# Row sums of a softmax: from matmuls with ones to a GpSimd fold and a VectorE reduction, in the second of two small-head attention layers

## What is computed

```
x = x + _L1_attn_ref(...)          # l1a: causal attention, 32 heads, 8 key heads, 8 channels a head
...
x = x + _L2_xattn_ref(_layernorm(x, axis=-1), ctx_2048, ctx_2048, mask_BxS2_if1,
                      L2_xattn_w_q, L2_xattn_w_k, L2_xattn_w_v, L2_xattn_w_o, L2_xattn_b_o)   # l2x
x = x + _L2_ffn_ref(_layernorm(x, axis=-1), L2_ffn_w_gate, L2_ffn_w_up, L2_ffn_w_down)        # l2f
```

## Time and profile before

| | us |
|---|---|
| median of 3 runs (1521.43 to 1523.54) | 1522.03 |
| profiled execution, its own time | 1525.09 |
| its span | 1523.3 |
| PE busy in the span | 1372.9 |
| DVE busy | 919.2 |
| ACT busy | 767.3 |
| POOL busy | 528.1 |

### The profile page before, as it was taken

How to read it: one execution, slowest core, us unless ns; L and a number is a source line. 1 busy time by engine, 2 the same in 40 slices (tenths; PEclk the granted TensorE clock), 3 DMA queues, 4 the chain that set the end, 5 groups by cost and what they waited for, 6 DMA issues and landing times.

```text
span 1523.3 us, 24834 instructions
## 1 busy us (share of the span) xinstructions
PE 1372.9 (90%) x9246; PEld 855.1 (56%) x9264; DVE 919.2 (60%) x1713; ACT 767.3 (50%) x1847; POOL 528.1 (35%) x528
## 2 busy tenths in 40 slices
PE   7869999999888879999999998998996789988799
PEld 3434555565455545666667774664663545545536
DVE  7784322224588755545555788855787587686631
ACT  3452111111788567776776456457776455363230
POOL 3230000000277468886882000110843435414200
PEclk9979999999999999999999999998998798988899
DMA  8020211001200300000000100020001100000100
GB/s 257 26 86 1 68 53 41 1 0 60 107 2 2 126 0 8 8 8 8 8 8 1 77 23 1 1 83 2 2 2 72 56 1 2 3 0 3 30 0 28
DMA packets 21851, 48.06 MB, mean 32 GB/s; under 512 B 1506, under 2 KB 16995, under 8 KB 20580
## 3 DMA queue, kind: packets, MB, share of 16 engines
q1 hardware_dynamic: 21732, 46.47, 8.9%
HBM read 41.22 MB, written 5.24 MB: 31 GB/s over the span
## 4 chain that ended last, share of the span: by engine, by line
PE 64%; DVE 21%; ACT 6%; issue 5%; POOL 4%; DMA 0%; DVEq 0%; ACTq 0%; POOLq 0%
PE PS L890 47%; PE PS L1128 5%; DVE work L2638 4%; PE PS L1187 3%; PE PS L891 3%; ACT work L1733 2%; PE PS L987 2%; PE PS L1225 2%; DVE small L2076 2%; DVE small L2425 1%; PE PS L904 1%; DVE work L2222 1%; DVE X L2617 1%; DVE work L2606 1%; POOL work L823 1%
## 5 line engine op out<-in xcount | busy, mean ns | idle before, releaser
L890 PE MATMUL PS<-XT,WB 128*128 128x512 f32 (+1 forms) x688 | 300.8, 595 | 5.2 <-DVE XT L2102 2.9
L890 PEld LDWEIGHTS PS<-XT,WB 128*128 128x128 f32 (+1 forms) x688 | 127.1, 191 | 149.8 <-issue 146.1
L1733 ACT ACTIVATE work<-PS,small 128x128 f32<-128x128 f32 x512 | 137.7, 416 | 43.6 <-DVE small L2425 43.6
L2297 DVE TENSOR_TENSOR work<-PS,work 128x512 f32<-128x512 f32 x48 | 33.1, 691 | 170.1 <-PE PS L890 170.1
L1659 ACT ACTIVATE work<-PS 128x512 f32<-128x512 f32 x48 | 28.7, 597 | 194.6 <-PE PS L890 194.6
L2425 DVE TENSOR_REDUCE small<-PS 128x4 f32<-128x512 f32 x128 | 80.5, 684 | 36.1 <-PE PS L890 34.6
L890 PE MATMUL PS<-XT,WA 128*128 128x512 f32 (+2 forms) x224 | 97.9, 600 | 4.4 <-DVE XT L2102 2.3
L666 POOL TENSOR_SCALAR small<-small 128x4 f32<-128x4 f32 x22 | 5.1, 230 | 268.3 <-DVE small L2079 268.2
L2638 DVE SCALAR_TENSOR_TENSOR work<-PS,vec,work 128x508 f32<-128x508 f32 (+2 forms) x108 | 80.2, 743 | 13.7 <-DVE work L2638 6.5
L1128 PE MATMUL PS<-WB,work 128*128 128x256 f32 x384 | 86.9, 379 | 0.5 <-DVE work L2302 0.5
L890 PE MATMUL PS<-WA,XT 128*128 128x256 f32 (+1 forms) x384 | 81.5, 374 | 3.6 <-DVE XT L2410 1.8
(11 more groups left out here) (388 smaller groups left out, 2988.3 us busy)
## 6 DMA issues: line engine op xcount, KB each, us to landing
WB<-in_l0f SPq DMA_DIRECT2D x8, 768.0 KB, 8.1
WB<-in_l1x SPq DMA_DIRECT2D x1, 6144.0 KB, 18.3
WB<-in_l0f SPq DMA_DIRECT2D x32, 96.0 KB, 7.2
WB<-in_l2f SPq DMA_DIRECT2D x1, 3072.0 KB, 10.0
WA<-in_l3a SPq DMA_DIRECT2D x1, 2624.0 KB, 9.3
WB<-in_l3f SPq DMA_DIRECT2D x1, 2064.0 KB, 7.9
WA<-in_l1f SPq DMA_DIRECT2D x1, 2056.0 KB, 11.2
C<-in_ctx SPq DMA_DIRECT2D x2, 1024.0 KB, 7.1
```

The source lines that it names most:

```text
L890: mm = lambda o, l, r, s, e: nc.tensor.matmul(o, l, r, start=s, stop=e)
L1733: f(wk(12288 + (u % 8) * G + h * P, P), bank(j)[:, h * P:(h + 1) * P], ACT.Exp, bias=sm(704 + (u % 8) * 4 + h, 1)).then_inc(*act_step(*([j ...
L2297: v.tensor_tensor(l0f_h(m)[:, lo:lo + G], bank(j), l0f_s(m)[:, lo:lo + G], ALU.mult).then_inc(*dve_step(j))
```

## The change

In `l2x` the 16 matmuls with ones of each group go, with the window of ones and its write on ACT. POOL makes one fold for each unit (128x512 exponentials to 128x256 sums of two), into columns of `XT` and `WA` that are free then. DVE reduces 64 columns a head of four units at once (128x1024 to 128x16), takes 16 reciprocals, spreads them, copies the product out of PSUM, and multiplies with the inverses of the group before from the bank of this group, as in `l1a`. ACT's exponentials of unit u wait for the fold of unit u-8, whose buffer they take. POOL's fold of unit u, from u = 8 on, waits for the inverses of group (u-8)//4, whose columns it takes. POOL's folds and the steps for `l2f`'s weights are put into one order by hand: the folds of rounds 0 to 7, then one weight step and the folds of one round in turn up to round 16, the folds of round 17, the roots, the folds of rounds 18 to 21. `rb` is now in both layers. The small tiles of sums and reciprocals move from `C` to `work` in both layers.

```
-        if sums_at is None:
-            l += [("rb", x) for x in (UNITS // 4 - 1,) if (4 * x + 3) // 3 + 3 == r]
+        l += [("rb", x) for x in (UNITS // 4 - 1,) if (4 * x + 3) // 3 + 3 == r]
...
-        def fold_once(u):
-            return C[:, (u % 2) * D:(u % 2 + 1) * D]
+        def fold_once(layer, u, n=1):
+            if layer == "l1a":
+                return C[:, (u % 2) * D:(u % 2 + 1) * D]
+            lo = u % 4 * D
+            return XT[:, N + lo:N + lo + n * D] if u % 8 < 4 else WA[:, 1664 + lo:1664 + lo + n * D]
...
+            def folds(*rounds):
+                for u in (u for r in rounds for u in round_of(r)):
+                    halves = r3(wk(12288 + (u % 8) * G, G), P)
+                    pool.wait_ge(*freed(job_of["l2x", "s", u]))
+                    if u >= 8:
+                        pool.wait_ge(*inverted("l2x", (u - 8) // 4))
+                    nc.gpsimd.tensor_tensor(r3(fold_once("l2x", u), 64), halves[:, :, 0:64], halves[:, :, 64:P], ALU.add).then_inc(folded_once, 1)
+            folds(*range(SUMS_AT + 1))
             pool.wait_ge(weight_scales, 1)
...
                     ins.then_inc(weights_ready, 1)
                     done += 1
+                    folds(SUMS_AT + done)
...
             for g in range(2):
+                folds(*(range(SUMS_AT + 10, QUANT_AT[0] // 3) if g == 0 else range(QUANT_AT[0] // 3, ROUNDS)))
                 pool.wait_ge(dve_to_pool.sem, dve_to_pool.next())
...
-                        if layer == "l1a" and x:
-                            pe.wait_ge(inverse_sums, x)
+                        if x:
+                            pe.wait_ge(*inverted(layer, x - 1))
                             nc.tensor.transpose(o[:, P:2 * P], inverse_spread(x - 1), cst("ident"))
-                        for part in range(1 if layer == "l1a" else 2):
...
-                f(ones_window[:, 24:32], cst("ones")[:, 0:8], ACT.Copy).then_inc(*act_step())
...
-                            if layer == "l1a":
-                                act.wait_ge(folded_once, u - 7)
+                            act.wait_ge(*folded(layer, u - 8))
...
+                else:
+                    dve.wait_ge(*folded(layer, 4 * x + 3))
+                    v.tensor_reduce(sums, r3(fold_once(layer, 4 * x, 4), 64), AX.X, ALU.add).then_inc(*dve_step())
...
-                        rs = wk(17920, P)
-                        v.reciprocal(rs, bank(j)[:, P:2 * P]).then_inc(*dve_step())
-                        v.tensor_tensor(XT[:, lo:lo + P], bank(j, P, P), rs, ALU.mult).then_inc(*dve_step(j))
+                        v.tensor_copy(XT[:, lo:lo + P], bank(j, P, P)).then_inc(*dve_step())
+                        if x:
+                            scaled_outputs(x - 1, j)
```

More of the change, by code:

```diff
@@ L472, in build, with inverse_job, folded, inverted @@
         keys_beside = WA[:, 5200:5456]
-        def fold_once(u):
-            return C[:, (u % 2) * D:(u % 2 + 1) * D]
+        def fold_once(layer, u, n=1):
[3 more added lines that the diff above has]
+            return XT[:, N + lo:N + lo + n * D] if u % 8 < 4 else WA[:, 1664 + lo:1664 + lo + n * D]
         def fold_twice(u, n=1):
             return C[:, 512 + (u % 8) * P:512 + (u % 8 + n) * P]
-        def inverse_job(x):
-            return job_of[("l1a", "pv", x + 1) if x + 1 < UNITS // 4 else ("l1a", "rb", x)]
+        def inverse_job(layer, x):
+            return job_of[(layer, "pv", x + 1) if x + 1 < UNITS // 4 else (layer, "rb", x)]
+        def folded(layer, u):
+            return folded_once, (UNITS if layer == "l2x" else 0) + u + 1
+        def inverted(layer, x):
+            return inverse_sums, (UNITS // 4 if layer == "l2x" else 0) + x + 1
         def inverse_spread(x):
@@ L997, in heads @@
                         pe.wait_ge(*freed(J(layer, "t", 4 * x + 3)))
-                        for part in range(1 if layer == "l1a" else 2):
[L999 to L1004, removed]
+                        for h in range(4):
+                            for k in range(4):
+                                u = 4 * x + k
+                                ins = mm(o[32 * k:32 * k + 32, 0:P], v_windows[:, u * 32 + 24 - 8 * h:u * 32 + 56 - 8 * h],
+                                         wk(8192 + (u % 8) * G + h * P, P), h == 0, h == 3)
                         end(ins)
                     elif key[0] == "rb":
-                        pe.wait_ge(inverse_sums, key[1] + 1)
+                        pe.wait_ge(*inverted(layer, key[1]))
                         end(nc.tensor.transpose(o[:, P:2 * P], inverse_spread(key[1]), cst("ident")))
@@ L1011, in heads @@
                         for x in range(4):
-                            pe.wait_ge(*freed(inverse_job(4 * bp + x) if layer == "l1a" else J(layer, "pv", 4 * bp + x)))
+                            pe.wait_ge(*freed(inverse_job(layer, 4 * bp + x)))
                         for i in range(2):
@@ L2392, in hidden_evac, with inverse_of @@
                 v.tensor_copy(XT[:, :].bitcast(BF16)[:, (b % 4) * 1024:(b % 4 + 1) * 1024], bank(j).bitcast(BF16)).then_inc(*dve_step(j))
[L2394 to L2398, removed]
+            def inverse_of(layer, x):
+                sums, inverse = wk(18176, 16), wk(18192, 16)
+                if layer == "l1a":
+                    dve.wait_ge(folded_twice, 4 * x + 4)
+                    v.tensor_reduce(sums, r3(fold_twice(4 * x, 4), 32), AX.X, ALU.add).then_inc(*dve_step())
+                else:
+                    dve.wait_ge(*folded(layer, 4 * x + 3))
+                    v.tensor_reduce(sums, r3(fold_once(layer, 4 * x, 4), 64), AX.X, ALU.add).then_inc(*dve_step())
                 dve.wait_ge(*dve_last())
```

32 lines of the change are left out of this document (10 added, 22 removed).

## The result

The changed kernel takes 1548.24 us (median of 4 runs, 1545.35 to 1549.99), the kernel before beside it 1522.78 us (4 runs, 1521.43 to 1523.72). The ratio is 1.0171, with a 95% interval of 1.0149 to 1.0193: slower, as forecast. The predicted 1544.1 is 4.1 us short of the median, and the median lies within the range of 1532 to 1552. The profiled execution took 1545.35 us (span 1543.6), 20.3 us more than the one of before (1525.09), where the sum said 22.1. So the profile read here is of the fastest of the four runs; the medians lie 25.5 us apart, and where the other 5 us went no trace shows.

A forecast was written before the change was run, and what follows sets the result against it. PE was taken as the second layer's bound, with POOL's queue deciding after the change. Roots 19.6 us later plus 2.5 behind them gave +22.1 us: 1547.2 profiled, 1544.1 median, range 1532 to 1552.

The forecast's parts named there:

- the sum: Whole kernel: 19.6 us from POOL's late roots plus 2.5 us behind them, +22.1 us in all.
- the queue followed: POOL from round 7 to the roots: folds and weight steps end at 1144.8, roots at 1146.1, 19.6 us later for DVE.
- PE's saving: PE's groups in the second layer: 0.55 us less each, 8.8 us for 16, nearly nothing of it reaching the end.
- The fold: POOL in the second layer: 0.74 us per fold, 47 us for 64; 0.72 gives -0.6 us, 0.82 gives +2.4.
- From there POOL waits for nobody.: POOL after round 8's folds, from 1082.75: eight weight steps of 42.04 us and folds of 19.98 run without waits to 1144.8.
- DVE's waits on the way: DVE waiting for POOL: some 5 us in rounds 15 and 17, some 8 us ahead of round 18, not added to 19.6.
- DVE's groups: DVE in the second layer: 1.00 us more per group; rounds with two copies 5.47 us for 5.06, 3.3 us for eight.
- the first rival: POOL's queue matters little and DVE sets the round: only longer groups count, +5 us, about 1527; chance 0.08.
- Rival 3: POOL and DVE slow each other: 38 POOL instructions 0.28 us longer each, train ends 10.6 us later, 1555; chance 0.05.
- From the roots to the end: Second layer behind POOL's roots, 28.8 us before: +1 for longer DVE groups, +1.5 for PE's clock, together +2.5 us.
- Rival 2: Faster: PE is and stays the bound of the second layer, which gets back 8.8 us, 1513; chance 0.07.

The follow-up runs named there:

- the first kernel above: The changed kernel with the nine weight steps on POOL cut to 4 of 2048 columns each: 1524.19 us, ratio 1.0017 to the kernel before.

## Why the prediction was right

The mechanism and the place were right: the folds stand with the weight steps in front of the root, and the first kernel above, without the weight steps, takes 18 of the 20 us back. How closely the place was met is in part luck. L2101 runs at 1146.04 where the queue followed said 1146.1, but round 7 lay 0.85 us earlier than in the trace before. Measured from round 7's maxima the queue gave 1146.12 - 1070.75 = 75.4 us (the prediction's own "some 76" doesn't follow from it), and the distance is 76.14, with two errors of opposite sign inside. And the prediction had named any idle time of POOL between rounds 9 and 17 as a sign of being wrong: there was one such wait. By the steps:

- *PE's saving.* 8.4 us of busy time for 8.8, and at the end of the kernel almost nothing. Alone, it is worth some 4 us. Round 7 began 0.85 us earlier than before, but the layer's first maxima were 0.52 us early already, so hardly any of it shows.
- *The fold.* 30 of them in the train take 21.3 us, 0.71 each, where I took 0.74 and bounded by 0.72 from below: a fold behind a fold starts some 0.69 us after it (2.79 for four). That is 0.9 us less than the sum's share.
- *"From there POOL waits for nobody."* Wrong by one wait, 1.95 us at 1099.90, for an inverse that a held copy had made late. This step failed, by the prediction's own sign. The wait is of the other sign than the fold's error, and so the distance to the root was missed by only 0.8 us. With the copy replaced, POOL does not idle there, and the distance is 74.1.
- *DVE's waits on the way.* This step failed in form. The waits of about 5 us in rounds 15 and 17 were not there (0.62 is the only one), and the one ahead of the root was 4.57 instead of 8. In their place stood the held copies. The sum did not feel it, since it had counted debt and not waits. With the copy replaced, the waits came out at 4.96, 3.67 and 8.04.
- *DVE's groups.* The round with two copies is 5.20 us for 5.47. Its price came out at 0.14 a round over the 5.06 of before, not 0.4, and the kernel without weight steps puts the whole of it at no more than +2.3 us in the stage, where the first rival had 5.
- *Rival 3,* that the two engines slow each other down, was more true than its 0.05 said, and by another law. I had priced it as 0.28 us more for each of POOL's instructions. What happens is that POOL isn't touched, and DVE's copy waits, with few exceptions, for the end of the POOL instruction that runs. Of the two readings of the earlier trace rows, the copy's 226 to 508 ns were the one to follow up: the folds there are short, so the hold was too. In the first layer of the kernel before, eight of the 16 copies begin within a fold, and each ends 0.08 or 0.09 us behind it. In the changed kernel the hold was worth about 2 us.
- *From the roots to the end.* 1176.90 - 1146.04 = 30.9 us for 28.8, +2.1 where +2.5 was forecast. The clock fell as expected; how much of the 2.1 is the clock's and how much the groups', no run tells. In the windows (PE's busy time first behind the length, granted clock third last, as in the earlier trace rows) PE is idle ahead of round 18's exponentials, and then works at 1.2 GHz (granted 0.50 and 0.52) before it is back at 2.4 (1.00):

```profile
1142.00:1148.00 6.00, 0.02 (x1) 0.00 (x0) 1.93 (x4) 1.77 (x4) 5.50 (x10) 0.80 0.00 0
1148.00:1152.00 4.00, 2.54 (x9) 0.79 (x9) 3.86 (x10) 3.87 (x14) 1.45 (x2) 0.50 0.00 0
1152.00:1156.00 4.00, 4.00 (x44) 2.46 (x39) 3.07 (x5) 2.28 (x10) 0.00 (x0) 0.52 0.00 0
1156.00:1160.00 4.00, 3.75 (x23) 2.70 (x24) 2.31 (x8) 1.91 (x6) 2.77 (x4) 1.00 0.02 4
```

- *What the profile does not hold.* The median is 4.1 us over the predicted one, and the profiled execution 1.9 us under the predicted 1547.2. The offset of 3.06 us between profile and median, taken over from the kernel before, had the other sign here (-2.9). Executions of one kernel differ by that much, and I have no cause for it. So the median, too, is met only within the spread: the loss between medians is 25.5 us, where the sum said 22.1.
- *Rival 2, faster.* Its price of 8.8 us was too large from the start: the kernel without the ones, where PE does even less, shows -4.3 us (-1.5 to -7.0), and that is all there was to be had.

## What to carry to other kernels

Work that is moved to an engine with room to spare on average has to be followed through that engine's queue: what stands in front of it, and what stands behind it that others need. Here 21 us of folds came to stand, beside 43 us of weight steps, ahead of a root of 1 us, and cutting the long steps into halves, dealing them out over the rounds and moving the root forward took back 17 to 19 of 25 us. What the change could save was some 4 us, which a kernel with the saving alone shows. And while GpSimd has long instructions running, look at what VectorE copies from SBUF to SBUF next to it: one short copy per group cost 10 us (6 to 14) in a kernel that was otherwise unchanged.

## What the hardware showed that was not expected

VectorE's SBUF-to-SBUF copy of 128x128 f32 (0.23 us) that begins within one of GpSimd's fp32 instructions of 128 to 2048 columns was held, in nearly all cases, until that one ended. It then lasted up to 4.88 us beside a clip of 7.08 (6.83 in the kernel with the root moved), and ended 0.08 us behind it; the clips of 2048 columns took 7.08 to 7.11 us with a held copy and 7.08 to 7.10 in the kernel before. Three copies went through in 0.23 us all the same: the one beside the root above, and two in the kernel with weight steps in halves. There six others were held to the end, and one of 0.63 us ended within a subtract. One of the two, and the clip of 1024 columns beside it:

```profile
1140.28 0.23 DVE L2435 COPY work<-work 128x128 f32<-128x128 f32 x1
```

```profile
1138.06 3.63 POOL L826 TENSOR_SCALAR WB<-WB 128x1024 f32<-128x1024 f32 x1
```

The clip beside the other, at 1084.18, took 3.72 us, where 3.63 is the median of six. What let these copies through is open.

A reduction over an axis of length 1, which writes the same 128x128 values from and to the same places, takes 0.29 us and was never held in 16 times, seven of them begun within a scale, clip or subtract. Nor were the copies that read PSUM, in 64 times (the copy L2463 of 2.66 us above, from PSUM too, stood behind a held one and ended with it):

```profile
L2454 DVE COPY work<-PS x64: 678/682/693, 409.5 to 1171.2; 128x512 f32<-128x512 f32 x64
```

Two pages of the Trainium skill have this, in two strengths. "GPSIMD Engine Reference" (Key points) speaks of contention with VectorE instructions in a two-port mode or with two SBUF inputs, and "Advanced Engine Details and Errata" (VectorE Performance Modes, Mode Summary) says that GPSIMD and two-port VectorE instructions will interfere with or block each other. Where a copy is held, the trace agrees with the second: it is a block, with waits up to 6.83 us. Only VectorE was seen to wait for long; what a copy of 0.23 us costs GpSimd is too little to be told. The copies that went through are not explained by either sentence. The reduction isn't held and the PSUM copies aren't, which fits a rule by port mode; that the mode is the reason is the page's word, and no run here shows it.
